# Gated cross-attention with a routed expert layer on one core: when GpSimd starts its indirect transfers

## The chip, the cores and the metric

The kernel runs on one core of one Trainium2 chip. The metric is the device time of one execution, in microseconds (us); less is better. Times shown for the kernel before are three such runs and one profiled execution.

## The reference

The inputs are x (64 sequences of 128 rows of 128 numbers), a context of 77 rows for each sequence, attention weights, a router and eight experts of two layers (128 to 256 to 128).

```python
x = x + tanh(g_xattn[0]) * xattn(layernorm(x), ctx, ctx, wq, wk, wv)
x = x + tanh(g_ffn[0]) * ffn(layernorm(x), Wr, br, W1, b1, W2, b2)
# xattn: 16 heads of depth 8
attn = softmax(einsum('bhqd,bhkd->bhqk', Q, K) / sqrt(8)); out = attn @ V
# ffn: the two best of eight experts for each row, gates = softmax over the two
h = relu(einsum('btd,edh->bteh', x, W1) + b1)
out = einsum('bte,bteh,ehd->btd', gates, h, W2) + einsum('bte,ed->btd', gates, b2)
```

## The kernel before, in words

Everything is written by hand for each engine, as a list of slots: `slots(slot)` calls each engine's `slot(t)` for t = 0, 1, 2, and so on. The engines agree through semaphores alone; each runs its own list in order, and an instruction that waits holds all that stand behind it on its engine.

**Attention.** Sequence b passes through the slots with fixed lags. In slot b+8 (`MAX_LAG`) TensorE makes four products of queries with keys, one for each group of four heads (`max_scores`, line 482, which counts semaphore p_max), only to find the largest score of each row; VectorE reduces each (`head_max`, line 1028, neg_max, semaphore s_max). These four share one PSUM bank from the fifth sequence on, so a product waits for the reduction of the one before it (lines 477 to 479). The maxima go through HBM into a spare row of the stacked queries. In slot b+13 (`SCORE_LAG`) TensorE makes the scores that count, four matmuls to each of four groups (`scores`, line 503, semaphore p_st), in two banks in turn; ScalarE takes their exponential (`exp_scores`, line 744), and TensorE multiplies it with the values (line 517). In slot b+14 the outputs are turned and added to x. So slot t works on the scores of sequence t-13 and on the maxima of sequence t-8, and in it TensorE's order is: scores 0, maxima 0, scores 1, maxima 1, turned outputs, values 0, scores 2, maxima 2, values 1, scores 3, maxima 3, values 2, values 3. Every fourth slot (t modulo 4 = 0) the first maxima product needs a fresh stack of queries, which SyncE loads in the slot before (`stack_q`, line 361).

**Experts.** 56 sequences are routed, in five chunks of 12, 12, 12, 12 and 8; the last eight sequences go through all experts densely (lines 615 to 651). For each routed sequence GpSimd starts two indirect transfers that scatter its 128 rows into tiles of one expert each in HBM (`scatter`, line 1347), SyncE loads the tiles turned, in quads of four (line 380), TensorE computes a quad in two halves (`hidden_part`, lines 591 to 593, semaphore p_hid), ScalarE applies bias and relu in four instructions to a half (`relu`, line 810, semaphore s_relu), and TensorE makes the outputs in the slot after (`rows_out`, lines 605 to 607). The outputs are stored, and GpSimd starts two indirect transfers for each sequence that gather them (`gather`, line 1362), which VectorE adds to x (lines 1205 and 1208). In a slot with a quad, TensorE's first half stands behind scores 0 and maxima 0, and its second half behind values 2, near the slot's end; both halves use one PSUM bank until slot 80, so each half waits for the relu of the half before it (line 582). A quad follows its last scatter by four slots and its first gather by three or more; the sums follow the gathers by four or five slots (lines 73 to 91).

**GpSimd's list.** It has little else to do: in slots with t modulo 4 = 0 it computes the first reciprocal deviations (line 1306, for t up to 64), in slots with t modulo 4 = 2 the second ones (line 1312), each waiting for a result of VectorE that comes at the end of the slot before or at the start of this one; then come the slot's transfers. The constants give two sequences, so four transfers, to each of these slots: 34 to 39, 46 to 51, 58 to 63 and 70 to 75 scatter; 53 to 57, 64 to 69 and 76 gather. From slot 78 on come the remaining 80 transfers. Quads stand in slots 43 to 50, 55 to 62, 67 to 73, 75 and 78 to 91.

**Pace.** `keep_pace(t, n, k)` (lines 1316 to 1333) stands ahead of every one of them; n is the sequence's number in the slot (0 or 1) and k the transfer's (0 or 1). Until slot 77 (`LAST_ATT` is 78) the transfer waits for TensorE to have made 4(t-13) + 2n + k groups of scores: the first transfer of a slot goes behind scores 3 of the slot before, the second behind scores 0 of this slot, the third behind scores 1 and the fourth behind scores 2. The waits keep transfers apart; the data that they need is held by other waits (lines 1338 to 1344, 1354 to 1359).

Of the kernel before, what the change touches and what calls it, by code (L numbers as in the profile page):

```python
# [18 lines left out]
MAX_LAG = 8  # L19
SCORE_LAG = 13  # L20
# [9 lines left out]
def clip(n, top):  # L30
    return max(0, min(n, top))


def flamingo_kernel(nc, x, ctx_t, g_xattn, g_ffn, w_att_t, w_router, b_router, w1, b1, w2, b2, out):
    B, S, D = x.shape
    NG, _, KEYS4 = ctx_t.shape
    NB = B // NG
    KEYS = KEYS4 // NB
    HEADS, DEPTH = 16, D // 16
    PER = 4  # L40
    HG = HEADS // PER
# [32 lines left out]
    t = 0  # L74
# [21 lines left out]
    t = GATED_ALL + 1  # L96
# [6 lines left out]
    with ExitStack() as stack:  # L103
# [3 lines left out]
        def sem(name):  # L107
            return stack.enter_context(nc.semaphore(name))
# [158 lines left out]
        p_max, p_st, p_pv, p_oT = (sem("pe_" + n) for n in ("max_scores", "scores", "values", "o_turned"))  # L267
# [7 lines left out]
        def active(s):  # L275
            return 0 <= s < B
# [8 lines left out]
        def quads_at(s):  # L285
            return [q for q in range(NQ) if QUAD_AT[q] == s]

        def quads_before(s):
            return len([q for q in range(NQ) if QUAD_AT[q] < s])
# [7 lines left out]
        def dense_before(s):  # L297
            return len([n for n in range(len(DENSE_AT)) if DENSE_AT[n] < s])
# [4 lines left out]
        def dense_at(s):  # L303
            return [n for n in range(len(DENSE_AT)) if DENSE_AT[n] == s]
# [123 lines left out]
        def _(pe):  # L428
# [131 lines left out]
            def name_weights(q):  # L560
                c = CHUNK_OF_QUAD[q]
                at_tile = 4 * (q - QUAD0[c])
                if at_tile == 0:
                    pe.wait_ge(s_rt, ROUTE * (c + 1))
                _, held[q] = nc.values_load_multi_w_load_instructions(
                    tile_w[c % 2][0:1, at_tile:at_tile + 4], engines=[mybir.EngineType.PE], min_val=0,
                    max_val=(E - 1) * HID, skip_runtime_bounds_check_because="DVE clamps the expert's number to 0..7")
# [152 lines left out]
        def _(act):  # L720
# [69 lines left out]
            def name_biases(q):  # L790
                c = CHUNK_OF_QUAD[q]
                at_tile = 4 * (q - QUAD0[c])
                if at_tile == 0:
                    act.wait_ge(s_rt, ROUTE * (c + 1))
                if q == 0:
                    act.wait_ge(s_b1c, 16)
                _, held[q] = nc.values_load_multi_w_load_instructions(
                    tile_b[c % 2][0:1, at_tile:at_tile + 4], engines=[mybir.EngineType.Activation], min_val=0,
                    max_val=(E - 1) * HC, skip_runtime_bounds_check_because="DVE clamps the expert's number to 0..7")
# [499 lines left out]
        def _(pool):  # L1299
# [13 lines left out]

            def keep_pace(t, n, k):
                if t < LAST_ATT:
                    pool.wait_ge(p_st, clip(HG * (t - SCORE_LAG) + 2 * n + k, HG * B))
                    return
                if quads_at(t):  # L1320
                    if n == 0:
                        pool.wait_ge(p_hid, 2 * quads_before(t) + k)
                    elif k == 0:
                        pool.wait_ge(p_y, quads_before(t))
                    else:
                        pool.wait_ge(p_hid, 2 * quads_before(t) + 2)
                if dense_at(t):
                    if n == 0:
                        pool.wait_ge(p_dhid, HC * dense_before(t) + k)
                    elif k == 0:  # L1330
                        pool.wait_ge(p_dhid, HC * dense_before(t) + HC)
                    elif dense_at(t - 1):
                        pool.wait_ge(p_dy, dense_before(t))

            def scatter(b, n):
                c, i = place_of(b)
                if i == 0:
                    if c < 2:
                        pool.wait_ge(s_clear[c], 16 * 8)
                    pool.wait_ge(s_rt, ROUTE * (c + 1))  # L1340
                    pool.wait_ge(s_rlo, (SEQ0[c] + CHUNKS[c]) // NB)
                    if c >= 2:
                        for q in range(QUAD0[c - 1] - 3, QUAD0[c - 1]):
                            pool.wait_ge(s_xs[q % 3], 32 * (q // 3 + 1))
                for k in range(2):
                    keep_pace(SCATTER_AT[b], n, k)
                    G.indirect_dma_start(out=xs_dram[c % 2], out_offset=bass.IndirectOffsetOnAxis(  # L1347
                        ap=at[k][c % 4][:, i:i + 1], axis=0), in_=rows[c % 2][:, i, :],
                        in_offset=None).then_inc(s_scat[c], 16)

            def gather(b, n):
                g = b // NB
                c, i = place_of(b)
                if i == 0:
                    last = QUAD0[c] + QUADS[c] - 1
                    for q in (last - 1, last):
                        pool.wait_ge(s_yst[q % 2], 16 * (q // 2 + 1))
                if b % NB == 0 and g >= 4:
                    pool.wait_ge(s_sum, NB * (g - 3))
                for k in range(2):  # L1360
                    keep_pace(ADD_AT[b], n, k)
                    G.indirect_dma_start(out=back[k][:, b % 16, :], out_offset=None,  # L1362
                                         in_=ys_dram[c % 2][0:TILES[c] * 128, :],
                                         in_offset=bass.IndirectOffsetOnAxis(ap=at[k][c % 4][:, i:i + 1], axis=0)
                                         ).then_inc(s_back[g], 16)
# [88 lines left out]
```

## Time and profile before

| | us |
|---|---|
| three runs, median | 694.86 |
| lowest and highest of them | 691.97, 694.98 |
| the profiled execution's own time | 691.36 |
| its span in the profile | 689.6 |
| busy PE, DVE, ACT, POOL | 571.9, 374.7, 362.9, 263.8 |
| granted TensorE clock, mean over the span | 0.935 of full speed |

PE is TensorE, DVE VectorE, ACT ScalarE, POOL GpSimd, SP SyncE; PEld is TensorE's weight loading, which runs beside its matmuls. An engine's busy time over the span says how full it is; what bounds a stretch is read from the chain of work, from the waits and from the order of instructions in time. A row of the timeline gives start, duration, engine, line, operation, written and read tiles, and in brackets how long the engine stood idle before it and what released it ("issue" is a release by nothing that the profile shows, "remote" one whose event is missing from the records). A matmul's end is modelled. POOL's row of an indirect transfer is the time in which it makes the descriptors, not that in which the data moves.

### The profile page before, as it was taken

How to read it: one execution, taken by the hardware profiler on the slowest of the kernel's cores; microseconds unless marked ns; L12 is line 12 of the kernel's file. 1: busy time of each engine (PE TensorE's matmuls, PEld its weight loads, DVE VectorE, ACT ScalarE, POOL GpSimd, SP SyncE). 2: the span in 40 equal slices, each digit the busy share in tenths (PEclk: the TensorE clock that was granted, in tenths of full speed). 3: DMA queues.
4: the chain of work that ended last, by engine and by line, in shares of the span. 5: the costliest groups of instructions: out<-in, count | busy, mean ns of one | idle time of the engine just before them, and what ended most of it. 6: DMA issues, size and time to landing. Idle time of an engine off the chain costs nothing.

```text
span 689.6 us, 18476 instructions
## 1 busy us (share of the span) xinstructions
PE 571.9 (83%) x6201; PEld 408.0 (59%) x6213; DVE 374.7 (54%) x1361; ACT 362.9 (53%) x835; POOL 263.8 (38%) x281
## 2 busy tenths in 40 slices
PE   2359998989788889999789899788886788899877
PEld 0225555545445566766466766466664588788656
DVE  4445866788656865445766555655543331242344
ACT  5215866655445566566466666355555345456222
POOL 6020010100664003443554445544445265556660
PEclk9967999999888999999999999899999689999999
DMA  4445545644433566654676554653432345674221
GB/s 117 115 117 146 136 111 138 151 103 122 143 97 114 102 105 121 129 97 137 128 118 128 126 117 144 90 125 87 98 100 81 69 97 144 116 163 125 77 79 48
DMA packets 158121, 78.65 MB, mean 114 GB/s; under 512 B 85088, under 2 KB 153312, under 8 KB 158032
## 3 DMA queue, kind: packets, MB, share of 16 engines
q1 hardware_dynamic: 119760, 45.65, 30.8%
q0 software_dynamic: 7168, 14.69, 9.3%
q10 hardware_dynamic: 31104, 17.13, 9.1%
q8 instruction: 54, 0.88, 0.6%
q14 instruction: 35, 0.29, 0.2%
HBM read 30.72 MB, written 36.75 MB: 98 GB/s over the span
## 4 chain that ended last, share of the span: by engine, by line
PE 65%; issue 9%; DVE 8%; ACT 6%; DMA 5%; another core or an unknown queue 3%; POOL 1%; ACTq 1%; SPq 1%; DVEq 0%; POOLq 0%
PE y L607 11%; PE bank_oT L517 9%; PE scores L503 8%; PE max_scores L482 6%; PE hidden_p L591 4%; PE o L530 3%; PE hidden_p L592 3%; DVE neg_max L1028 3%; DMA q_st<-q_dram 3%; PE hidden_p L593 3%; PE max_scores L541 2%; ACT probs L744 2%; ACT hidden L810 2%; PE o L648 2%
## 5 line engine op out<-in xcount | busy, mean ns | idle before, releaser
L1028 DVE TENSOR_REDUCE neg_max<-max_scores 128x4 f32<-128x308 f32 x244 | 116.3, 476 | 154.4 <-PE max_scores L482 145.7
L744 ACT ACTIVATE probs<-scores 77x512 f32<-77x512 f32 x256 | 148.6, 596 | 66.3 <-PE scores L503 63.1
L1347 POOL DMA_INDIRECT xs_dram<-rows,at x112 | 109.4, 977 | 92.1 <-PE scores L503 71.9
L1362 POOL DMA_INDIRECT back<-ys_dram,at x112 | 107.0, 955 | 90.0 <-PE scores L503 44.2
L517 PE MATMUL bank_oT<-probs,v_cols 77*9 77x128 f32 x2048 | 108.0, 286 | 11.5 <-ACT probs L744 8.0
L482 PE MATMUL max_scores<-k_st,q_st 128*128 128x308 bf16 x244 | 77.5, 317 | 40.1 <-DVE neg_max L1028 17.1
L503 PE MATMUL scores<-q_st,k_st 128*77 128x128 bf16 x1024 | 109.4, 233 | 0.2
L503 PEld LDWEIGHTS scores<-q_st,k_st 128*77 128x77 bf16 x1024 | 75.0, 121 | 50.1 <-issue 41.7
L810 ACT ACTIVATE hidden<-hidden_p,b_cols 128x128 f32<-128x128 f32 x256 | 73.5, 369 | 55.5 <-PE hidden_p L593 40.7
L607 PE MATMUL y<-w_sb,hidden 128*128 x608 | 96.6, 299 | 0.0
L607 PEld LDWEIGHTS y<-w_sb,hidden 128*128 128x128 f32 x608 | 84.5, 201 | 2.7
L591 PE MATMUL hidden_p<-xsT,w_sb 128*128 128x128 bf16 x256 | 53.6, 229 | 15.7 <-ACT hidden L810 10.7
L819 ACT COPY ys<-y 128x512 f32<-128x512 f32 x38 | 22.3, 588 | 79.3 <-PE y L607 60.8
L517 PEld LDWEIGHTS bank_oT<-probs,v_cols 77*9 77x9 f32 x2048 | 30.6, 89 | 56.5 <-issue 26.4
L1306 POOL TENSOR_TENSOR rstd<-ve,power 128x4 f32<-128x4 f32 x16 | 16.4, 1026 | 114.6 <-DVE ve L969 91.1
L1312 POOL TENSOR_TENSOR rstd<-ve,power 128x4 f32<-128x4 f32 x16 | 17.7, 1106 | 111.0 <-DVE ve L996 111.0
L482 PEld LDWEIGHTS max_scores<-k_st,q_st 128*128 128x128 bf16 x244 | 24.8, 101 | 50.7 <-DVE neg_max L1028 25.3
L592 PE MATMUL hidden_p<-xsT,w_lo 128*128 128x128 bf16 x256 | 52.7, 223 | 0.4 <-issue 0.4
L593 PE MATMUL hidden_p<-xsT,w_sb 128*128 128x128 bf16 x256 | 52.9, 223 | 0.0
L738 ACT COPY oT<-bank_oT 128x512 f32<-128x512 f32 x64 | 37.6, 587 | 24.9 <-PE bank_oT L517 14.4
L530 PE MATMUL o<-ident,oT 128*128 128x128 f32 x256 | 42.6, 293 | 5.8 <-ACT oT L738 5.7
L591 PEld LDWEIGHTS hidden_p<-xsT,w_sb 128*128 x256 | 25.4, 99 | 32.1 <-issue 27.5
(144 smaller groups left out, 928.7 us busy)
## 6 DMA issues: line engine op xcount, KB each, us to landing
ys_dram<-ys ACTq DMA_DIRECT2D x38, 256.0 KB
q_st<-q_dram SPq DMA_DIRECT2D x16, 512.0 KB
k_st<-k_dram SPq DMA_DIRECT2D x64, 77.0 KB
xs_all<-x SPq DMA_DIRECT2D x16, 256.0 KB, 4.1
q_dram<-q_hl SPq DMA_DIRECT2D x16, 256.0 KB
xs_dram<-zeros_b ACTq DMA_DIRECT2D x16, 256.0 KB, 3.4
out<-xs_all SPq DMA_DIRECT2D x16, 256.0 KB
k_dram<-k_hl SPq DMA_DIRECT2D x48, 77.0 KB
```

Of the source, the lines that this page charges most:

```text
L482: mm(max_to(b, h)[:, 0:PER * KEYS], q_st[g % 3][:, h, seq_cut(b, S)], k_st[g % 3][:, h, b % NB, :, :].rearrange("p j k -> p (j k)"), start ...
L503: last = mm(score_bank[h % 2][0:KEYS, j * S:(j + 1) * S], k_st[g % 3][:, h, b % NB, j, :], q_st[g % 3][:, h, seq_cut(b, S)], start=True, s ...
L517: last = mm(oT_bank[ROWS * j:ROWS * j + VW, h * S:(h + 1) * S], v_cols[g % 3][:, b % NB, h * PER + j, :], probs[h][:, j * S:(j + 1) * S], ...
L591: mm(o, w_hi[:, at_w], tiles[:, 0, cut], start=True, stop=False, skip_group_check=True)
L592: mm(o, w1_lo[:, at_w], tiles[:, 0, cut], start=False, stop=False, skip_group_check=True)
L593: last = mm(o, w_hi[:, at_w], tiles[:, 1, cut], start=False, stop=True, skip_group_check=True)
L607: last = mm(o, hidden[:, (2 * q + t // 2) % 4, t % 2, m, :], w2_sb[:, bass.ds(w + m * 128, 128)], start=False, stop=(m == HC - 1), skip_gr ...
L744: nc.scalar.activation(probs[h][:], score_bank[h % 2][0:KEYS, :], ACT.Exp, scale=SCALE).then_inc(s_exp, 1)
L810: last = nc.scalar.activation(hidden[:, k % 4, i, m, :], of[:, j * 128:(j + 1) * 128], ACT.Relu, bias=b1_cols[:, bass.ds(held[q][2 * half ...
L1028: V.tensor_reduce(neg_max[:, i // 2, :, h, i % 2], max_to(b, h)[:, 0:PER * KEYS].rearrange("p (j k) -> p j k", j=PER), AXIS_X, ALU.max, ne ...
L1347: G.indirect_dma_start(out=xs_dram[c % 2], out_offset=bass.IndirectOffsetOnAxis(ap=at[k][c % 4][:, i:i + 1], axis=0), in_=rows[c % 2][:, i ...
L1362: G.indirect_dma_start(out=back[k][:, b % 16, :], out_offset=None, in_=ys_dram[c % 2][0:TILES[c] * 128, :], in_offset=bass.IndirectOffsetO ...
```

## The change

In slots whose maxima products exist (t-8 is a sequence, so up to slot 71), the first transfer of each pair (k = 0) waits for 4(t-8) + 2n products for the maxima, and the second of the pair (k = 1) waits for nothing: the first pair goes behind the fourth product of the slot before, the second pair behind the second product of this slot. In slots 72 to 77 the pairs keep the scores' count, again with a wait for k = 0 alone. From slot 78 on nothing changes. No other line is touched.

```diff
             def keep_pace(t, n, k):
+                if active(t - MAX_LAG):
+                    if k == 0:
+                        pool.wait_ge(p_max, HG * (t - MAX_LAG) + 2 * n)
+                    return
                 if t < LAST_ATT:
-                    pool.wait_ge(p_st, clip(HG * (t - SCORE_LAG) + 2 * n + k, HG * B))
+                    if k == 0:
+                        pool.wait_ge(p_st, clip(HG * (t - SCORE_LAG) + 2 * n, HG * B))
                     return
```

## Rows read from the trace of the kernel before

**Rows 1.** The page's busy times, shares of the span and instructions
```profile
PE 571.9 (83%) x6201; PEld 408.0 (59%) x6213; DVE 374.7 (54%) x1361; ACT 362.9 (53%) x835; POOL 263.8 (38%) x281
```

**Rows 2.** The page's chain that ended last, by line
```profile
PE y L607 11%; PE bank_oT L517 9%; PE scores L503 8%; PE max_scores L482 6%; PE hidden_p L591 4%; PE o L530 3%; PE hidden_p L592 3%; DVE neg_max L1028 3%; DMA q_st<-q_dram 3%; PE hidden_p L593 3%; PE max_scores L541 2%; ACT probs L744 2%; ACT hidden L810 2%; PE o L648 2%
```

**Rows 3.** Windows: slots 28-33, 34-39, 58-62, 63-66; length, busy (count), PE clock, DMA
```profile
136.00:173.40 37.40, 32.25 (x395) 20.03 (x395) 32.34 (x125) 21.29 (x43) 2.82 (x3) 0.95 0.47 115
173.40:220.30 46.90, 36.31 (x383) 22.42 (x382) 28.04 (x99) 21.87 (x45) 27.59 (x28) 0.82 0.43 125
...
372.80:421.20 48.40, 43.95 (x536) 33.29 (x534) 26.54 (x92) 30.28 (x81) 22.99 (x24) 1.00 0.54 129
421.20:452.70 31.50, 26.26 (x289) 17.16 (x290) 19.56 (x73) 14.49 (x32) 16.70 (x18) 0.84 0.60 121
```

**Rows 4.** Timeline of POOL, slots 36 and 37
```profile
194.97 0.96 POOL L1347 DMA_INDIRECT xs_dram<-rows,at  x1 [1.21 <-PE scores L503]
196.23 0.96 POOL L1347 DMA_INDIRECT xs_dram<-rows,at  x1 [0.30 <-issue]
198.46 0.96 POOL L1347 DMA_INDIRECT xs_dram<-rows,at  x1 [1.28 <-PE scores L503]
```

**Rows 5.** Timeline of PE and DVE beside these transfers
```profile
196.44 0.29 PE L482 MATMUL max_scores<-k_st,q_st 128*128 128x308 bf16 x1
...
198.25 0.48 DVE L1028 TENSOR_REDUCE neg_max<-max_scores 128x4 f32<-128x308 f32 x1 [1.90 <-PE max_scores L482]
...
198.79 0.30 PE L482 MATMUL max_scores<-k_st,q_st 128*128 128x308 bf16 x1 [1.83 <-issue]
```

**Rows 6.** Timeline of PE, POOL and DVE in slot 62, which has a quad
```profile
412.85 0.29 PE L482 MATMUL max_scores<-k_st,q_st 128*128 128x308 bf16 x1
...
413.01 0.97 POOL L1347 DMA_INDIRECT xs_dram<-rows,at  x1 [0.30 <-issue]
...
414.61 0.48 DVE L1028 TENSOR_REDUCE neg_max<-max_scores 128x4 f32<-128x308 f32 x1 [2.79 <-PE max_scores L482]
```

**Rows 7.** Timeline of POOL: first and last transfer behind another, slots 34 to 76
```profile
177.14 0.96 POOL L1347 DMA_INDIRECT xs_dram<-rows,at  x1 [0.31 <-issue]
...
533.10 0.95 POOL L1362 DMA_INDIRECT back<-ys_dram,at  x1 [0.30 <-issue]
```

**Rows 8.** Timeline of POOL, slot 59: its first and second transfer
```profile
378.72 0.97 POOL L1347 DMA_INDIRECT xs_dram<-rows,at  x1 [0.70 <-PE scores L503]
381.31 0.97 POOL L1347 DMA_INDIRECT xs_dram<-rows,at  x1 [1.62 <-PE scores L503]
```

**Rows 9.** Timeline of PE and DVE behind the second of these
```profile
382.99 0.29 PE L482 MATMUL max_scores<-k_st,q_st 128*128 128x308 bf16 x1
...
383.33 0.48 DVE L1028 TENSOR_REDUCE neg_max<-max_scores 128x4 f32<-128x308 f32 x1 [1.45 <-PE max_scores L482]
```

**Rows 10.** Timeline of PE and ACT, from slot 58's second half to slot 59's first
```profile
378.28 0.29 PE L482 MATMUL max_scores<-k_st,q_st 128*128 128x308 bf16 x1
...
380.02 0.22 PE L593 MATMUL hidden_p<-xsT,w_sb 128*128 128x128 bf16 x1
...
380.38 0.63 ACT L810 ACTIVATE hidden<-hidden_p,b_cols 128x128 f32<-128x128 f32 x2 [1.02 <-PE hidden_p L593]
...
381.78 0.23 PE L591 MATMUL hidden_p<-xsT,w_sb 128*128 128x128 bf16 x1 [0.62 <-ACT hidden L810]
```

**Rows 11.** Waits of PE, slots 34-39: what waited for what, us in total, times, longest
```profile
PE max_scores L482 <- DVE neg_max L1028: 4.7, 3, 3.0
PE max_scores L482 <- issue: 4.3, 4, 1.8
```

**Rows 12.** The same for slots 63 to 66
```profile
PE max_scores L482 <- issue: 2.6, 2, 1.6
PE max_scores L482 <- DVE neg_max L1028: 2.2, 2, 1.7
```

**Rows 13.** The load of the stacked queries, line 361: who waited for it
```profile
  PE max_scores L482: 12.3, 5
```

## The prediction

> **What bounds the kernel now.** I read the page first. TensorE is busy for 83% of the span and GpSimd for 38% [rows 1], and the chain that ended last runs mostly over TensorE's lines with reductions and exponentials between them [rows 2]. Indirect transfers stand nowhere on that chain. So a transfer can only matter through what it does to the others, and the next view was the windows. Slots 28 to 33 and 34 to 39 differ in little but the 24 scatters: without them six slots take 37.4 us, with them 46.9 us, and the TensorE clock granted falls from 0.95 to 0.82 [rows 3]. Some 1.6 us a slot go somewhere. Slots 58 to 62, with scatters and quads, take 9.7 us each at a full clock, with TensorE busy for 43.95 of 48.4 us [rows 3]: little is left to win there, and much can be lost.
>
> The timeline shows where it goes. TensorE's product for the maxima begins at 196.44 and is done at 196.73; VectorE is idle, waits for nothing else, and starts its reduction at 198.25, 1.5 us late, whereupon TensorE has waited 1.83 us for its next product [rows 5]. In that time lies a transfer that began at 196.23, 0.30 us behind the end of the one before it [rows 4]; GpSimd itself, which waits for a count of TensorE's, also got it only for its start at 198.46 [rows 4]. The same in a slot with quads: transfer at 413.01 straight behind another, product done at 413.14, reduction at 414.61, 1.5 us late [rows 6]. Behind a transfer that stands alone it isn't so: it begins at 381.31 [rows 8], the next product is done at 383.28 and the reduction starts at 383.33, 0.05 us later [rows 9]. Going through slots 34 to 76 I find 144 transfers, 41 of which begin 0.3 us behind another's end (from 177.14 to 533.10 [rows 7]). Of the reductions that start over 0.6 us behind their product, all but one have such a transfer running or just ended. I read this as a **hold**: for about 1.6 us from the start of the second of two adjoining transfers, TensorE's counts reach nobody. What holds them no row shows; the coincidence and its length I take from the rows.
>
> **The parts of the change.** (1) Waits: of the 144 transfers, 72 lose theirs. The wait itself costs GpSimd alone 0.3 us or less, and GpSimd isn't on the chain: nothing. (2) The second of each pair now always starts 1.26 us behind the first (1.26 is 196.23 less 194.97 [rows 4]). Adjoining transfers go from 41 to at least 72. (3) The first pair goes behind maxima 3 instead of scores 3, about 0.1 us later; the second pair behind maxima 1 instead of scores 1, the same; the second of each comes earlier by 0.5 to 1.5 us. (4) Nothing of the data is late: quads follow scatters by four slots, sums follow gathers by four, SyncE's loads and the two small power operations behind GpSimd's waits come no later. No DMA issue is added.
>
> *Slots with quads.* Rows 10 show the handover that a held count hits: TensorE ends the second half of a quad at 380.24, ScalarE starts the relu at 380.38, and TensorE, idle for 0.62 us, starts the next quad at 381.78 as soon as the relu is done (1.4 us later). Now put the pair in. Maxima 3 of slot 58 ends at 378.57 [rows 10]; GpSimd starts 0.28 us after such a count (378.85), its second transfer 1.26 later, at 380.11, and the hold lasts to 381.7. The count of 380.24 falls into it. The relu starts at 381.7 instead of 380.38: TensorE idles 1.3 us more. Before, the second transfer began at 381.31 only [rows 8], behind the relu. This fits where the slot before has a quad, this one too, and GpSimd doesn't begin with a power operation, which already delays the first pair and makes it adjoining: slots 47, 49, 57, 59, 61, 69, 71, 72, 73. Nine places; some relus there wait a little today, so I take 1.2 each, an estimate from the 1.3: **11 us**. The ends: 0 if the hold reaches only the maxima, 9 x 1.6 = 14 if it lasts longest. The second pair holds maxima 2's count by some 0.8 us; products lie 2.35 us apart in such slots (maxima 3 begins at 378.28 [rows 10], maxima 1, two products on, at 382.99 [rows 9]) and a reduction takes 0.48 [rows 9], so that is covered. If that cover were gone, 20 such slots would lose up to 0.8 each.
>
> *Slots without quads* (34 to 39, 53, 54, 64 to 66). Here a held reduction stops TensorE at once [rows 5]. But most of these transfers adjoin already, since GpSimd runs behind and finds its counts met: by my count as many as pairs would make, but for one more in each of 36, 38, 54, 64 and 66, where four in a row take the place of three. One more member lengthens the hold by 1.26 us: at most 5 x 1.26 = 6.3 us. From below: the holds also move, and one may fall where nothing waits, -4 us. Nearest to what the rows show is a small loss, since the single that it replaces has a short hold too: **2 us**.
>
> Sum: 11 + 2 = 13 us on the profiled execution's 691.36, so 704.4. The median of the three runs stands 3.5 us above that execution; on it the sum gives 707.9. I say **707**, between the two and nearer the median, which is what will be compared.
>
> **A rule against the rows.** VectorE's reduction starts 1.5 us behind a finished product while GpSimd makes descriptors [rows 5, 6]. The Trainium skill ("SBUF — State Buffer", "Who interferes with whom") says that only VectorE and GpSimd share an SBUF port, that a reduction never contends on trn2, and that TensorE and ScalarE wait on nobody. By that rule pairing costs nothing and the time would stay at 695. The rows disagree with it for the handover, though it may hold for ports; it is the second rival.
>
> **Rivals.**
> *Fewer holds (faster).* Perhaps what counts is how often GpSimd disturbs, not whether transfers adjoin: four scattered starts a slot become two bursts, each behind a product whose count has already passed. In the slots without quads TensorE waits ahead of the maxima's products for 4.7 + 4.3 us [rows 11] and 2.6 + 2.2 us [rows 12], 13.8 us in ten slots. Halved that is 7 us: 688. It decides at the first pair: from there on it wins if the hold of a pair ends before scores 0 and maxima 0 are done. Against it: in slot 36 and 37 the pairs are exactly where the waits are [rows 4, 5].
> *No effect.* Adjoining transfers may be the result and not the cause: something else holds TensorE's counts, GpSimd falls behind, and catches up in pairs. For it: GpSimd waits for these counts too. Against it: at 413.01 the pair comes from the power operation and the late VectorE, and the hold follows all the same [rows 6]. 695. The port rule above gives the same time.
> *Bursts ahead of the queries' load (slower).* TensorE waits 12.3 us for line 361 in five places [rows 13]. A pair puts two transfers' data at once on the DMA engines, in the slot in which that load runs. If each of the eight groups concerned waited 0.5 us more, that is 4 us: 699. Against it: the DMA share is only about 0.5 [rows 3].
>
> **How the numbers follow.** About 0.5% (3.5 us) is what a measurement can tell from no change. Forecast: 0.57, of which 0.55 is slower by more than that. Fewer holds: 0.20 (0.16 faster, 0.04 same). No effect: 0.13 (0.11 same, 0.01 to each side). Bursts: 0.10 (0.07 slower, 0.03 same). That makes faster 0.17, same 0.20, slower 0.63. The forecast's own range goes from 698 (the holds hit half of the nine places, and slots without quads win a little) to 716 (14 + 6.3 on the median, 715.2). Down to 689 it takes in no effect, bursts and a third of fewer holds; about 0.1 is left out below and 0.07 above.
>
> **What would show it.** Right: POOL's rows in pairs 1.26 us apart, two to a slot; in slots 47, 59, 61 the relu's first row starts 1.4 us or more behind the last row of line 593, and line 591 of the next quad waits 1.5 to 2 us for ACT; VectorE's idle time ahead of neg_max grows; slots 58 to 62 take about 10.2 us on average instead of 9.7. Wrong: if the relu starts within 0.2 us inside a pair, there is no hold of that kind; if slots 34 to 39 fall below 46 us, fewer bursts are what counts; if the first maxima product of every fourth slot waits longer for line 361, it is the bursts. If p_max reaches GpSimd much later than 0.28 us behind the product, the pair moves off the relu and the 11 us shrink.

## The result, and the profile after

The changed kernel takes 734.62 us (median of 6 runs, 729.12 to 737.98), the kernel before 694.92 us (6 runs beside it, 691.95 to 701.19). The ratio is 1.0562, with an interval of 1.0496 to 1.0628: **slower by 39.7 us**. The forecast had the sign and the kind of loss, but a third of its size (707.0, range 689 to 716). The profiled execution of the changed kernel took 731.33 us, with a span of 729.6 us.

The page of the changed kernel, its busy times, its clock row (forty slices of the span) and four of its groups (line, engine, operation, busy time and mean ns, then the idle time before them and what ended most of it):

```profile
PE 589.6 (81%) x6201; PEld 421.4 (58%) x6213; DVE 373.9 (51%) x1361; ACT 363.4 (50%) x835; POOL 265.1 (36%) x281
...
PEclk9969999997779998999899999699988879999999
...
L1028 DVE TENSOR_REDUCE neg_max<-max_scores 128x4 f32<-128x308 f32 x244 | 116.1, 476 | 186.8 <-PE max_scores L482 155.7
...
L1353 POOL DMA_INDIRECT xs_dram<-rows,at x112 | 109.7, 980 | 107.1 <-PE max_scores L482 54.9
...
L810 ACT ACTIVATE hidden<-hidden_p,b_cols 128x128 f32<-128x128 f32 x256 | 73.5, 369 | 70.3 <-PE hidden_p L593 51.6
...
L591 PE MATMUL hidden_p<-xsT,w_sb 128*128 128x128 bf16 x256 | 55.0, 234 | 26.1 <-ACT hidden L810 23.7
```

The numbers of instructions on TensorE, VectorE, ScalarE and GpSimd are those of [rows 1]: no work was added. TensorE is busy for 589.6 us instead of 571.9, with the same 6201 matmuls: 17.7 us of the loss are matmuls that take longer, not idle time.

TensorE's waits over the whole span (what waited, for what: us in total, times, longest), of the kernel before:

```profile
PE max_scores L482 <- DVE neg_max L1028: 17.1, 26, 3.0
...
PE max_scores L482 <- DMA q_st<-q_dram: 12.3, 5, 5.2
PE hidden_p L591 <- ACT hidden L810: 10.7, 12, 1.7
PE max_scores L482 <- issue: 9.6, 10, 1.8
...
PE hidden_p L591 <- issue: 5.0, 4, 1.8
```

And of the changed one:

```profile
PE max_scores L482 <- DVE neg_max L1028: 31.0, 36, 4.7
PE hidden_p L591 <- ACT hidden L810: 23.7, 14, 2.5
PE max_scores L482 <- DMA q_st<-q_dram: 12.9, 6, 4.8
...
PE hidden_p L591 <- issue: 2.3, 2, 1.5
...
PE max_scores L482 <- issue: 1.9, 3, 1.2
```

The wait of a quad's first half for the relu before it grows by 13.0 us, the wait for the reduction by 13.9. Part of both stood under "issue" before: with it the idle time ahead of line 591 grows from 15.7 to 26.0 us, by 10.3, and that ahead of line 482 from 26.7 to 32.9 us, by 6.2. The load of the queries stays where it was.

Where in the kernel: a slot's time runs here from the first row of line 744 in it to the first of the next slot. Sums of six slots, in us, of the profiled executions:

| slots | 34-39 | 40-45 | 46-51 | 52-57 | 58-63 | 64-69 | 70-75 | from 76 on |
|---|---|---|---|---|---|---|---|---|
| before | 46.8 | 46.8 | 55.9 | 49.9 | 56.0 | 51.6 | 53.7 | 155.5 |
| changed | 50.5 | 45.6 | 64.0 | 55.2 | 64.0 | 57.2 | 63.9 | 155.9 |

Slot 34 starts at 173.4 us in both, slot 76 at 534.1 and 573.7: all of it comes in the stretch that the rule touches, and most where quads stand beside transfers. Each row is one profiled execution: slots 34 to 39 take 46.8 us here and 48.0 us in the trace of the nine places below, where their pace is the same, so a difference of a microsecond in one column says nothing. Windows of slots 58 to 63 of the kernel before (length, busy time and count of PE, PEld, DVE, ACT and POOL, granted clock, DMA share, GB/s):

```profile
372.80:428.80 56.00, 51.41 (x622) 39.05 (x621) 30.23 (x108) 35.04 (x90) 26.06 (x28) 1.00 0.53 131
```

The same of the changed kernel:

```profile
388.60:452.60 64.00, 54.33 (x622) 41.85 (x621) 30.07 (x107) 34.92 (x90) 26.08 (x28) 0.95 0.46 115
```

The same 622 matmuls: 2.9 us more busy at a clock of 0.95 instead of 1.00, and 5.1 us more idle (64.00 less 54.33 is 9.67; 56.00 less 51.41 is 4.59).

**One place, row by row.** The handover from slot 60's quad to slot 61's, timeline of the kernel before (start, duration, engine, line, tiles, and in brackets the idle time and its releaser):

```profile
400.86 0.22 PE L593 MATMUL hidden_p<-xsT,w_sb 128*128 128x128 bf16 x1
...
401.21 0.63 ACT L810 ACTIVATE hidden<-hidden_p,b_cols 128x128 f32<-128x128 f32 x2 [1.01 <-PE hidden_p L593]
...
402.04 0.97 POOL L1347 DMA_INDIRECT xs_dram<-rows,at  x1 [1.50 <-PE scores L503]
...
402.61 0.23 PE L591 MATMUL hidden_p<-xsT,w_sb 128*128 128x128 bf16 x1 [0.72 <-ACT hidden L810]
```

and of the changed kernel:

```profile
418.76 0.97 POOL L1353 DMA_INDIRECT xs_dram<-rows,at  x1 [3.26 <-PE max_scores L482]
...
419.92 0.22 PE L593 MATMUL hidden_p<-xsT,w_sb 128*128 128x128 bf16 x1
...
420.03 0.97 POOL L1353 DMA_INDIRECT xs_dram<-rows,at  x1 [0.30 <-issue]
...
421.93 0.63 ACT L810 ACTIVATE hidden<-hidden_p,b_cols 128x128 f32<-128x128 f32 x2 [2.67 <-remote]
...
423.33 0.23 PE L591 MATMUL hidden_p<-xsT,w_sb 128*128 128x128 bf16 x1 [2.37 <-ACT hidden L810]
```

The transfer that came at 402.04, behind the relu, now starts at 420.03, 1.27 us behind its partner and 0.11 us before the quad's last product is done. The relu starts 1.79 us behind that product's end instead of 0.13, and TensorE idles for 2.37 us instead of 0.72. ("remote" stands where the trace has no record of the release.) Then comes what the forecast had not in its sum. Window of the next 4 us, kernel before:

```profile
402.70:406.70 4.00, 4.00 (x48) 3.50 (x49) 2.09 (x8) 2.23 (x7) 1.34 (x3) 1.00 0.82 212
```

And the changed one:

```profile
423.40:427.40 4.00, 4.00 (x29) 3.76 (x30) 1.35 (x5) 2.24 (x7) 1.48 (x2) 0.57 0.68 150
```

TensorE is never idle in either, but does 29 matmuls instead of 48, at a granted clock of 0.57: most of that stretch lies at 1.2 GHz, behind an idle time of 2.37 us, while behind 0.72 us the clock stayed at 2.4 GHz. Slot 61, which begins with these rows, takes 10.63 us instead of 9.14.

### The profile page after: what moved, and what is told of

It reads as the page before. It is cut to its first block, busy times and chain, and to the rows that moved or that the text cites. A ratio compares the mean times of both kernels' runs of the same rounds, so it can differ in the third digit from the quotient of the medians.

```text
span 729.6 us, 18476 instructions
## 1 busy us (share of the span) xinstructions
PE 589.6 (81%) x6201; PEld 421.4 (58%) x6213; DVE 373.9 (51%) x1361; ACT 363.4 (50%) x835; POOL 265.1 (36%) x281
## 4 chain that ended last, share of the span: by engine, by line
PE 60%; issue 9%; DVE 9%; DMA 6%; ACT 6%; another core or an unknown queue 5%; POOL 1%; SPq 1%; ACTq 1%; DVEq 0%; POOLq 0%
PE y L607 11%; PE bank_oT L517 7%; PE scores L503 7%; PE max_scores L482 5%; DMA q_st<-q_dram 4%; PE hidden_p L593 4%; PE o L530 3%; PE hidden_p L591 3%; DVE neg_max L1028 3%; PE hidden_p L592 3%; ACT probs L744 2%; PE max_scores L541 2%; PE o L648 2%; PE bank_oT L648 2%
## 5 line engine op out<-in xcount | busy, mean ns | idle before, releaser
L1028 DVE TENSOR_REDUCE neg_max<-max_scores 128x4 f32<-128x308 f32 x244 | 116.1, 476 | 186.8 <-PE max_scores L482 155.7
L517 PE MATMUL bank_oT<-probs,v_cols 77*9 77x128 f32 x2048 | 109.8, 289 | 16.7 <-ACT probs L744 12.0
L503 PE MATMUL scores<-q_st,k_st 128*77 128x128 bf16 x1024 | 111.9, 237 | 0.2
L810 ACT ACTIVATE hidden<-hidden_p,b_cols 128x128 f32<-128x128 f32 x256 | 73.5, 369 | 70.3 <-PE hidden_p L593 51.6
L503 PEld LDWEIGHTS scores<-q_st,k_st 128*77 128x77 bf16 x1024 | 77.2, 124 | 51.1 <-issue 44.7
L607 PE MATMUL y<-w_sb,hidden 128*128 x608 | 101.7, 309 | 0.0
L607 PEld LDWEIGHTS y<-w_sb,hidden 128*128 128x128 f32 x608 | 89.4, 211 | 3.3
L591 PE MATMUL hidden_p<-xsT,w_sb 128*128 128x128 bf16 x256 | 55.0, 234 | 26.1 <-ACT hidden L810 23.7
L593 PE MATMUL hidden_p<-xsT,w_sb 128*128 128x128 bf16 x256 | 54.7, 230 | 0.0
L592 PE MATMUL hidden_p<-xsT,w_lo 128*128 128x128 bf16 x256 | 54.3, 228 | 0.0
L530 PE MATMUL o<-ident,oT 128*128 128x128 f32 x256 | 45.9, 310 | 7.2 <-issue 4.1
```

Source lines behind the costliest of these rows:

```text
L503: last = mm(score_bank[h % 2][0:KEYS, j * S:(j + 1) * S], k_st[g % 3][:, h, b % NB, j, :], q_st[g % 3][:, h, seq_cut(b, S)], start=True, s ...
L517: last = mm(oT_bank[ROWS * j:ROWS * j + VW, h * S:(h + 1) * S], v_cols[g % 3][:, b % NB, h * PER + j, :], probs[h][:, j * S:(j + 1) * S], ...
L591: mm(o, w_hi[:, at_w], tiles[:, 0, cut], start=True, stop=False, skip_group_check=True)
L592: mm(o, w1_lo[:, at_w], tiles[:, 0, cut], start=False, stop=False, skip_group_check=True)
L593: last = mm(o, w_hi[:, at_w], tiles[:, 1, cut], start=False, stop=True, skip_group_check=True)
L607: last = mm(o, hidden[:, (2 * q + t // 2) % 4, t % 2, m, :], w2_sb[:, bass.ds(w + m * 128, 128)], start=False, stop=(m == HC - 1), skip_gr ...
```

## The experiments

The theory after the result: a transfer that starts 1.27 us behind another holds back TensorE's counts; what matters is that distance, not which count releases a pair or how many waits there are; and each place costs the idle time and the clock that falls behind it. Its rivals: the loss comes from the maxima as releaser; from the data of two transfers at once; from a transfer that starts close ahead of a count that matters, whatever its distance from the one before; or all of it is hold and none of it clock. Ratios are to the kernel before on the same chip, whose medians were 692.25 us (13 runs) for the first four, 691.54 us (19) for the next four and 693.54 us (19) for the last four.

**First pair apart** and **second pair apart.** The change, but with its rule on one pair only; the other pair's transfers each wait for scores as before. The first of the two:

```diff
-                if active(t - MAX_LAG):
+                if active(t - MAX_LAG) and n:
...
-                    if k == 0:
-                        pool.wait_ge(p_st, clip(HG * (t - SCORE_LAG) + 2 * n, HG * B))
+                    if n == 0 or k == 0:
+                        pool.wait_ge(p_st, clip(HG * (t - SCORE_LAG) + 2 * n + k, HG * B))
```

(The second has `n == 0` in the first condition and `n or k == 0` in the other.)

> The first two transfers of a slot wait for scores one by one as in the kernel before; the second two stay a pair behind maxima 1. Theory (an adjoining transfer holds TensorE's counts, which costs most where the held count is the one that releases a quad's relu, and TensorE's clock falls behind the long idle time): the first pair carries the loss in slots with quads, so 698 to 706, no half-clock stretches in slots 46 to 51 and 58 to 63. Rival (the number of pairs counts, wherever they are): half of the 40 us back, about 715. Rival (waiting for the maxima's count costs): also about 715.

> The mirror image: the first two transfers of a slot are a pair behind maxima 3 of the slot before, the second two wait for scores one by one. Theory: 722 to 732, nearly the changed kernel's 735, with the relu of a quad's second half late in slots 47, 49, 57, 59, 61, 69, 71 to 73. Rival (number of pairs): about 715.

Measured: with only the second pair tied 699.84 us, 1.0114 (1.0031 to 1.0196); with only the first pair tied 729.59 us, 1.0519 (1.0440 to 1.0597). The first pair carries 37 us, the second 8; together they are a little more than the whole change. Slots 58 to 63 take 56.9 us with the second pair alone against 56.0 before, so there the second pair is nearly covered, as the forecast had it. It isn't everywhere: slots 46 to 51 take 57.6 us instead of 55.9, at a clock of 0.97 instead of 1.00, where no slow stretch was expected, and the 20 slots with quads from 46 to 73 together 5.2 us more in that trace. Half of this, 2.6 us, stands in slots 46, 50, 58, 62 and 70.

**Maxima for each** and **scores in pairs.** The two halves of the rule: the other semaphore without pairs, and pairs without the other semaphore. Against the kernel before:

```diff
+                if active(t - MAX_LAG):
+                    pool.wait_ge(p_max, HG * (t - MAX_LAG) + 2 * n + k)
+                    return
```
```diff
-                    pool.wait_ge(p_st, clip(HG * (t - SCORE_LAG) + 2 * n + k, HG * B))
+                    if k == 0:
+                        pool.wait_ge(p_st, clip(HG * (t - SCORE_LAG) + 2 * n, HG * B))
```

> Every transfer keeps a wait of its own, but for the count of the maxima's products instead of the scores': 4(t-8) + 2n + k. Theory: what counts is that transfers adjoin, not which product they follow 0.1 us later: 693 to 698, as the kernel before. Rival (the place behind the maxima is what costs): over 710.

> Pairs as in the changed kernel, but behind the scores' counts of the kernel before (k = 0 alone waits). Theory: 728 to 738, as the changed kernel. Rival (the place behind the maxima): under 705.

Measured: 689.95 us, 0.9992 (0.9952 to 1.0032), and 727.97 us, 1.0501 (1.0436 to 1.0566); both lie just under the times expected. The semaphore is worth nothing that can be measured; the interval of the pairs overlaps that of the whole change. GpSimd's rows of slots 36 and 37 with scores in pairs (the first line is the power operation of slot 36):

```profile
187.39 1.04 POOL L1306 TENSOR_TENSOR rstd<-ve,power 128x4 f32<-128x4 f32 x1 [3.03 <-DVE ve L969]
188.63 1.03 POOL L1349 DMA_INDIRECT xs_dram<-rows,at  x1 [0.20 <-issue]
189.97 0.96 POOL L1349 DMA_INDIRECT xs_dram<-rows,at  x1 [0.30 <-issue]
191.24 0.96 POOL L1349 DMA_INDIRECT xs_dram<-rows,at  x1 [0.31 <-issue]
192.50 0.96 POOL L1349 DMA_INDIRECT xs_dram<-rows,at  x1 [0.30 <-issue]
194.91 0.95 POOL L1349 DMA_INDIRECT xs_dram<-rows,at  x1 [1.45 <-remote]
196.17 0.96 POOL L1349 DMA_INDIRECT xs_dram<-rows,at  x1 [0.30 <-issue]
```

Behind a power operation both pairs find their counts met and run as four. Of 143 transfers between the starts of slots 34 and 76 those that start less than 1.35 us behind another's start are 38 before, 36 with maxima for each, 76 with scores in pairs and 76 in the changed kernel (3 more of the kernel before and 5 more of the changed one start 1.35 to 1.6 us behind another's; with them it is 41 and 81).

**A gap inside the pairs.** The change, with a memset by GpSimd ahead of every transfer with k = 1 whose slot lies before 78, in two lengths (700 and 250 columns; `ADD_AT[b]` in the gathers):

```diff
+                    if k and SCATTER_AT[b] < LAST_ATT:
+                        if gaps:
+                            pool.wait_ge(s_gap, len(gaps))
+                        G.memset(idle_b[:, 0:700], 0.0).then_inc(s_gap, 1)
+                        gaps.append(n)
```

> The changed kernel, with a memset of a scratch tile of 700 bf16 columns on GpSimd between the two transfers of every pair (slots 34 to 77), and no wait: the two start about 2 us apart instead of 1.26. Theory (the hold comes of a transfer that starts before the one ahead of it has got rid of its descriptors and data, so of the distance): most of the 40 us comes back, 696 to 706. Rival (a transfer whose start waits for nothing of TensorE's holds the counts, at any distance): 730 or more.

> The same with 250 columns, so that the two start about 1.6 us apart. Theory: the first transfer's short hold ends some 1.45 us behind its start, so 1.6 is just enough and the time is near that of the long gap, under 712. If the hold needs a full 2 us, 725 or more.

Measured: the long gap 694.73 us, 1.0066 (1.0026 to 1.0105); the short gap 713.74 us, 1.0350 (1.0275 to 1.0426). A pair with the long gap, timeline of POOL:

```profile
204.14 0.96 POOL L1360 DMA_INDIRECT xs_dram<-rows,at  x1 [0.30 <-issue]
205.10 0.69 POOL L1357 MEMSET idle_b<- 128x700 bf16 x1
205.97 0.96 POOL L1360 DMA_INDIRECT xs_dram<-rows,at  x1 [0.17 <-issue]
```

And one with the short gap:

```profile
198.19 0.95 POOL L1360 DMA_INDIRECT xs_dram<-rows,at  x1 [2.64 <-PE max_scores L484]
199.14 0.33 POOL L1357 MEMSET idle_b<- 128x250 bf16 x1
199.63 0.97 POOL L1360 DMA_INDIRECT xs_dram<-rows,at  x1 [0.16 <-issue]
```

Starts 1.83 us apart give nearly all of the loss back, a little more than was expected, and starts 1.44 us apart some 0.4 of it, which lies between the two outcomes expected. The first is a net result: slots 34 to 39 take 43.2 us instead of the 46.8 of the kernel before, slots 58 to 63 take 59.9 instead of 56.0. GpSimd is busier with the memsets, and the waits, the releasers and the order are those of the change. But the gap also moves the second transfer later: at the handover to slot 61 it now starts 0.78 us behind the quad's last product, where in the changed kernel it started 0.11 us ahead of it. These two runs alone can't tell its distance from its place.

The rows of all fourteen traces together can. For slots 34 to 75, take every reduction, relu and exponential that starts after its engine has idled for 0.3 us or more and was idle already when TensorE's last product for it was done. Sort them by how far the latest transfer stands behind the one before it, and by when the product was done after that transfer's start. The table has the number that start over 0.6 us behind their product, and of how many:

| latest transfer starts behind the one before by | product done 0 to 0.4 us after its start | 0.4 to 0.8 us | 0.8 to 1.2 us | over 2 us |
|---|---|---|---|---|
| under 1.35 us | 87 of 98 | 62 of 77 | 75 of 105 | 0 of 363 |
| 1.35 to 1.6 us | 16 of 33 | 32 of 39 | 3 of 11 | 0 of 72 |
| 1.6 to 2 us | 1 of 35 | 17 of 30 | 21 of 70 | 0 of 233 |
| over 2 us | 0 of 13 | 5 of 36 | 16 of 45 | 0 of 296 |

At the same place behind a transfer's start, the distance decides: a product done in the first 0.4 us is late behind a close neighbour and on time behind a lone transfer. A lone transfer holds counts too, but only those made from some 0.4 us after its start, and until about 1.5 us after it.

Nor is it the data of two transfers at once. The trace's packet records (32 packets of GpSimd's queue to a transfer) have the data of the two transfers of 418.76 and 420.03 in the changed kernel at 420.32 to 420.67 and at 421.86 to 422.68; between these, when the relu still waits, none of either moves.

**Busy while it waits.** The change, with 30 matmuls that are no part of the reference's work, into a bank that nobody reads then, ahead of the first half of the quads of ten slots, so that TensorE has something to do while the relu is held:

```diff
+                if quads_at(t) and quads_at(t - 1) and t in (47, 49, 57, 59, 61, 68, 69, 71, 72, 73):
+                    q = quads_at(t)[0]
+                    pe.wait_ge(s_ys, q - 1)
+                    pe.wait_ge(s_place, ranks_before(QUAD_AT[q - 1] + 1))
+                    for _ in range(30):
+                        mm(y_bank[:, 0:128], ident_b[:], ident_b[:], start=True, stop=True, skip_group_check=True)
```

> The changed kernel, with 30 matmuls of 128 columns in bf16, whose output is overwritten, on TensorE ahead of a quad's first half in slots 47, 49, 57, 59, 61, 68, 69, 71, 72 and 73: they fill TensorE's idle time while the relu is held and are no work of the reference. Theory (a part of the loss is TensorE at half clock behind these idle times, 1.5 us at each): no half-clock stretches there and 716 to 724 instead of 735. Rival (the idle times alone make the loss): 733 to 740.

Measured: 713.51 us, 1.0359 (1.0275 to 1.0443), by work added. Against 1.0562 that is 2.0% of the kernel before, some 14 us back; the raw medians, 734.62 and 713.51 us, differ by 21 us, but the kernel before took 694.92 us beside the one and 691.54 beside the other. The two profiled executions agree with the 14: slots 34 to 75 take 386.3 us instead of 400.3, with TensorE busy for 334.2 us, 19.8 of them the added matmuls, instead of 327.3. So its own matmuls take some 13 us less, and its time without work of the reference is the same within a microsecond or so. The handover to slot 61, timeline:

```profile
410.57 0.97 POOL L1359 DMA_INDIRECT xs_dram<-rows,at  x1 [0.30 <-issue]
...
411.39 1.84 PE L677 MATMUL y<-ident_b 128*128 128x128 bf16 x30
412.34 0.63 ACT L816 ACTIVATE hidden<-hidden_p,b_cols 128x128 f32<-128x128 f32 x2 [2.54 <-remote]
...
413.75 0.23 PE L591 MATMUL hidden_p<-xsT,w_sb 128*128 128x128 bf16 x1 [0.52 <-ACT hidden L816]
```

And the 4 us behind it, window:

```profile
413.80:417.80 4.00, 4.00 (x48) 3.50 (x49) 1.31 (x5) 2.25 (x7) 1.94 (x2) 1.00 0.74 159
```

The relu is as late as in the changed kernel (1.77 us behind the second transfer's start, there 1.90), but the clock stays at 1.00 and the next 4 us hold 48 matmuls again. Four slots around it, in us, with the kernel before and the one after next:

| slot | before | changed | busy while it waits | nine places |
|---|---|---|---|---|
| 58 | 9.01 | 10.80 | 10.59 | 10.39 |
| 59 | 10.49 | 12.00 | 10.52 | 12.15 |
| 60 | 10.34 | 11.99 | 11.84 | 11.92 |
| 61 | 9.14 | 10.63 | 9.17 | 10.75 |

The idle time of a handover falls at the end of the slot ahead (58, 60), its slow clock into the slot behind (59, 61). The filling matmuls take away the second and leave the first: this place is some 1.6 us of idle time and 1.5 us of clock. They don't do so at every place: slot 47 takes 11.83 us with them and 11.79 in the changed kernel.

**Nine places.** The kernel before, but in the nine slots that the forecast named the second transfer follows the first without a wait. **Pairs where no quad stands.** The kernel before, with pairs in the slots without quads only.

```diff
-                    pool.wait_ge(p_st, clip(HG * (t - SCORE_LAG) + 2 * n + k, HG * B))
+                    if not (n == 0 and k == 1 and t in (47, 49, 57, 59, 61, 69, 71, 72, 73)):
+                        pool.wait_ge(p_st, clip(HG * (t - SCORE_LAG) + 2 * n + k, HG * B))
```
```diff
-                    pool.wait_ge(p_st, clip(HG * (t - SCORE_LAG) + 2 * n + k, HG * B))
+                    if k == 0 or quads_at(t):
+                        pool.wait_ge(p_st, clip(HG * (t - SCORE_LAG) + 2 * n + k, HG * B))
```

> The kernel before, but in slots 47, 49, 57, 59, 61, 69, 71, 72 and 73 the second transfer waits for nothing: nine adjoining transfers more, at the place where the prediction put its 11 us. Theory, as the changed kernel's trace has it (1.7 us of idle TensorE and 1.5 us at half clock behind it, at each): 715 to 722. If the prediction's 1.2 us a place were right: 701 to 705. If the relu is not where it hurts: 690 to 697.

> The kernel before, but pairs (k = 0 alone waits, for scores) in the slots without a quad: 34 to 39, 51, 53, 54, 63 to 66, 74 and 76. Theory: most of these transfers adjoin already, so 694 to 702. Rival (these slots carry a good half of the 40 us): over 708.

Measured: nine places 719.25 us, 1.0363 (1.0289 to 1.0436), which is 25.7 us for nine transfers that start earlier, 2.9 us each; the 4 us behind the same handover, window:

```profile
420.80:424.80 4.00, 4.00 (x29) 3.74 (x29) 1.30 (x5) 2.19 (x7) 0.97 (x1) 0.59 0.70 150
```

What the nine places cost in idle time and what in clock is read from the windows of slots 34 to 75, of the kernel before, the changed one and the nine places:

```profile
173.40:534.10 360.70, 310.31 (x3704) 220.31 (x3702) 208.25 (x764) 205.84 (x505) 158.85 (x162) 0.95 0.52 114
...
173.40:573.70 400.30, 327.33 (x3704) 233.66 (x3702) 207.43 (x764) 206.24 (x505) 159.46 (x162) 0.91 0.46 102
...
177.90:562.80 384.90, 325.56 (x3704) 232.77 (x3702) 208.38 (x764) 205.99 (x506) 157.87 (x162) 0.91 0.48 106
```

All do the same 3704 matmuls. The nine places add 24.2 us here: 15.3 us in which TensorE is busy longer at a lower clock, 1.7 a place, and 8.9 us of idle time (59.3 instead of 50.4), 1.0 a place. The changed kernel adds 17.0 us of the first and 22.6 of the second. How far single traces differ by themselves: the maxima for each, worth nothing in the medians, are busy for 309.9 us there and idle for 48.1.

Pairs in the other slots 704.27 us, 1.0161 (1.0113 to 1.0208), 10.7 us, above the range expected; whether it is as much as 2% slower is unclear. The two sum to 36.4 of the 39.7 us. Of the 10.7 us, 2.5 come in slots 34 to 39; slots 50 and 62 to 64, where a pair stands in the slot behind a run of quads, give 5.3 (from 8.85, 9.32, 7.69 and 8.14 us to 10.14, 10.06, 9.28 and 9.83), and slots 73 to 75 another 2.6. In slots 50, 62 and 73 it is again the relu of the quad's second half that is held: it starts 1.43, 1.34 and 1.22 us behind its product, where the kernel before has 0.14, 0.51 and 0.58. Of the whole 13.7 us that slots 34 to 75 take longer in this trace, 8.7 are TensorE busy longer (319.0 us) and 5.0 idle time.

**The other way: no neighbours at all.** If distance is what counts, the kernel before should gain from gaps as well. Kernel before, with the memset (450 columns) ahead of every transfer of a slot before 78; then only in slots without quads; then in those and the late slots from 78 on:

```diff
+                    if SCATTER_AT[b] < LAST_ATT:
...
+                        G.memset(idle_b[:, 0:450], 0.0).then_inc(s_gap, 1)
```
```diff
+                    if SCATTER_AT[b] < LAST_ATT and not quads_at(SCATTER_AT[b]):
```
```diff
+                    if SCATTER_AT[b] >= LAST_ATT or not quads_at(SCATTER_AT[b]):
```

> The kernel before (every transfer waits for its scores), with a memset of 450 columns on GpSimd ahead of each transfer of slots 34 to 77, so that none adjoins another: two starts are at least 1.7 us apart. Theory: the 41 adjoining transfers of the kernel before cost it time too, most in the slots without quads: 678 to 688. Rival (in those slots GpSimd only catches up, and any transfer holds as much): 691 to 697.

> The kernel before with the memset of 450 columns ahead of each transfer only in slots without a quad (34 to 39, 51, 53, 54, 63 to 66, 74, 76). Theory: the gain that the gaps brought in slots 34 to 39, 53, 54 and 66 stays (12 us in one trace) and the losses in slots with quads, where GpSimd fell behind, go: 679 to 685. Rival (the gain is given back in the slots behind): 687 to 692.

> The same, and the memset ahead of each of the 80 transfers from slot 78 on too. Theory: many of those adjoin as well, so 2 to 8 us less than with gaps in the slots without quads alone. Rival (there the gathers themselves are late, and the gaps delay them): more than that.

Measured: everywhere 688.14 us, 0.9940 (0.9905 to 0.9975); only without quads 688.19 us, 0.9911 (0.9876 to 0.9947); with the late slots 693.00 us, 1.0000 (0.9962 to 1.0037). The first lies at the edge of what was expected, the other two do not reach it. POOL's timeline with gaps everywhere:

```profile
187.97 0.96 POOL L1354 DMA_INDIRECT xs_dram<-rows,at  x1 [0.17 <-issue]
188.93 0.49 POOL L1351 MEMSET idle_b<- 128x450 bf16 x1
189.58 0.97 POOL L1354 DMA_INDIRECT xs_dram<-rows,at  x1 [0.16 <-issue]
```

The window of slots 34 to 39 with gaps only where no quads stand, to be read against the second line of [rows 3]:

```profile
175.50:214.00 38.50, 33.22 (x383) 20.44 (x382) 28.05 (x98) 22.36 (x45) 34.36 (x46) 0.91 0.52 147
```

The same 383 matmuls in 38.5 us instead of 46.9, with GpSimd busier by 6.8 us; TensorE's wait for the reduction is 3.1 us there instead of 4.7 + 4.3 [rows 11]. Of these 8.4 us, 3.1 are TensorE's own matmuls at a clock of 0.91 instead of 0.82, the rest idle time, and together they are nearly the whole price of the 24 scatters in [rows 3]. But the kernel gains only 0.9%, since most comes back later: with gaps everywhere a transfer takes 1.61 us of GpSimd, which falls behind (slot 67 goes from 9.11 to 12.98 us); with gaps only where no quads stand, slot 55 goes from 8.37 to 12.16 us, slot 64 from 8.14 to 9.60 and slot 67 from 9.11 to 10.49. The expectations of 679 to 685 us and of a further gain in the late slots were both too hopeful. The version with gaps where no quads stand is the only one whose whole interval lies 0.5% or more under the kernel before, and it takes 6% less time than the changed kernel.

## Why the forecast was right in kind and wrong in size

**The hold: right, from a weak control.** The forecast read from [rows 5, 6] that the second of two neighbouring transfers holds TensorE's counts. Pairs alone (1.0501), the releaser alone (0.9992), the pairs with a long gap (1.0066) and the table of late starts bear it out. Transfers less than 1.6 us behind another went from 41 to 81; "at least 72" was said. But the row that was to show that a lone transfer holds nothing, [rows 8, 9], has its product done 1.97 us after the transfer's start, when even the hold of a close neighbour would be over. The table shows that a lone transfer has a hold too, a shorter one.

**The nine places: right places and right idle time, but the clock was put at nothing. This is the step that failed.** "I take 1.2 each", 11 us, with 14 as the upper end. Nine places done alone cost 25.7 us, 2.9 each. The idle time in it is what was forecast: 8.9 us in the trace, 1.0 each, less than the 1.65 us that it came to at the place shown above in the changed kernel. What is missing is what TensorE does behind the idle time: 15.3 us, 1.7 each, of the same matmuls at a lower clock. [rows 3] had the sign of it, a clock of 0.82 in slots with waits and 1.00 in slots 58 to 62, and the forecast quoted both, yet priced the places as if the clock would stay at 1.00. It fell behind 2.37 us of idle time and had not behind 0.72, and it stayed at 1.00 where matmuls filled the idle time. The Trainium skill ("TensorE: Matmul & The Clock Gate", "What's actually happening") says that the clock is throttled by default and that activity releases it; the trace agrees. With 8.9 + 15.3 in place of 11 the forecast would have been 720.

**Slots without quads: too small, for the same reason and one more.** "2 us", at most 6.3, where pairs there alone cost 10.7. The idle time among it, 5.0 us, lies within that range; 8.7 us of clock do not stand in it. And the count went by runs of four in place of three. It left out the places where such a slot stands behind a quad: slots 51, 63 and 74, whose pair at the start holds the relu of the slot ahead. In slots 34 to 39 the loss is 2.5 us with pairs there and 3.6 us in the changed kernel, where two traces of the same pace differ by 1.2.

**The second pair beside quads is covered: mostly right** (56.9 against 56.0 us for slots 58 to 63 with that pair alone, but 5.2 us in 20 such slots, where 16 was the most it could be). **Waits, maxima instead of scores, data: right**, nothing that can be measured.

**The rivals.** *Fewer holds*: ruled out; slots 34 to 39 went up, from 46.8 to 50.5 us. *No effect*, and with it the rule on SBUF ports (the Trainium skill, "SBUF — State Buffer", "Who interferes with whom"): the measurement differs from 695 by 40 us. That rule may hold for ports, since nothing here shows that a port is what holds the counts; read as a rule that TensorE's work is undisturbed by GpSimd it would mislead. *Bursts ahead of the queries' load*: 12.3 us became 12.9, not the mechanism.

**The checks named ahead.** Pairs 1.26 us apart: 1.27, yes. The relu 1.4 us or more behind line 593: 1.41 at slot 59 and 1.79 at slot 61, but 0.86 at slot 47. The next quad's wait of 1.5 to 2 us: 2.37 at slot 61. VectorE's idle time ahead of neg_max: 186.8 us instead of 154.4. Slots 58 to 62 at 10.2 us: 11.3 (56.3 over five, 8.0 more than before). These 8.0 are three lots of idle time (slots 58, 60 and 62: 1.8, 1.65 and 1.6) and two of the slow clock (59 and 61: 1.5 each), where the forecast had two places at 1.2.

## What to carry to other kernels

Where a product's count hands work from TensorE to another engine and back, keep indirect transfers from starting close behind one another there: look in the timeline for starts 1.3 us apart and for counts that arrive late beside them, and let something stand between the starts. When pricing an added wait on TensorE, add what the clock costs in the stretch behind it, with a stretch of the same trace at each clock as the measure: here it cost more than the wait. And a stall taken out in one stage (8.4 us here) is worth only what the next stages do not give back.

## What the runs showed of the hardware

- An indirect transfer that GpSimd starts 1.27 us behind another holds back TensorE's counts to ScalarE, VectorE and GpSimd itself until up to 1.9 us after its start, although TensorE goes on with matmuls that wait for nothing (420.67 us, a maxima product, in the changed kernel's trace) and GpSimd's own row is 0.97 us long. At starts 1.44 us apart about 0.6 of the loss remains, at 1.83 us little. A lone transfer holds fewer counts, until about 1.5 us after its start (1.49 us at a relu of the long gap's kernel, whose transfer stands 5.21 us behind another). That it is the counts that are held, and not the engines that receive them, is inferred from several engines being late at once:

```profile
420.67 0.29 PE L482 MATMUL max_scores<-k_st,q_st 128*128 128x308 bf16 x1
...
422.01 0.48 DVE L1028 TENSOR_REDUCE neg_max<-max_scores 128x4 f32<-128x308 f32 x1 [2.28 <-PE max_scores L482]
```

  The trace's own records of the semaphores (no view prints them) agree: the counts of the relu's product, the values, the scores and the maxima of this handover come at 421.80, 421.90, 421.95 and 421.99 us, within 0.2 us, for matmuls that began at 419.92, 420.06, 420.44 and 420.67. Whether counts of the other engines are held as well stays open, since a part of their records is missing beside transfers. What holds the counts stays open too; no run here tells descriptor making, the queue and the events apart.
- At one handover 1.65 us more of idle time cost another 1.5 us through the clock, in 4 us in which TensorE was never idle. Over nine such places alone, 8.9 us of idle time brought 15.3 us of clock.
- Useless matmuls in place of idle time took 2.0% off the time, some 14 us (1.0562 became 1.0359).
